# Decoder layer, one core: the experts' first norm moved into cross attention, x2 stored a batch later, the experts' steps reordered

## The reference

```
x = layernorm(x + self_attention(x, relative position bias))
x = layernorm(x + cross_attention(x, ctx, ctx))
x = layernorm(x + ffn(x))
ffn: aff = x @ centroids.T (8 experts); e = argmax(aff); alpha = sigmoid(aff[e])
     h  = relu((layernorm(x) * g[e] + b[e]) @ w1[e].T + b1[e])   # 256 -> 1024
     ye = x + h @ w2[e].T + b2[e];   out = alpha * ye + (1 - alpha) * x
```

## Time and profile before

| | us |
|---|---|
| median of 3 runs (lowest, highest) | 1068.13 (1065.26, 1069.1) |
| the profiled execution: its time | 1071.02 |
| its span, first to last instruction | 1069.2 |
| PE, ACT, DVE, POOL busy over the span | 942.3, 772.8, 675.9, 347.9 |
| mean granted TensorE clock | 0.937 of full |

### The profile page before, as it was taken

How to read it: one execution, slowest core, us unless ns; L and a number is a source line. 1 busy time by engine, 2 the same in 40 slices (tenths; PEclk the granted TensorE clock), 3 DMA queues, 4 the chain that set the end, 5 groups by cost and what they waited for, 6 DMA issues and landing times. The chain is left out here.

```text
span 1069.2 us, 17528 instructions
## 1 busy us (share of the span) xinstructions
PE 942.3 (88%) x5301; PEld 523.5 (49%) x5301; DVE 675.9 (63%) x1760; ACT 772.8 (72%) x1452; POOL 347.9 (33%) x340
## 2 busy tenths in 40 slices
PE   5599999999999999999999999962599889898891
PEld 2233444444444433333333333321599779888790
DVE  5276877777777777354546464753377667667672
ACT  1387777787877868899989898940478767686670
POOL 4043133140313111001112211221436666665664
PEclk9699999999999989999999999985699999898895
DMA  8988587978769576695587558400523334333441
GB/s 210 201 229 235 120 249 143 320 153 243 201 154 275 103 195 109 148 266 110 123 151 153 105 117 160 100 20 28 197 91 119 105 110 176 105 117 115 127 169 44
DMA packets 73546, 162.93 MB, mean 152 GB/s; under 512 B 16441, under 2 KB 40056, under 8 KB 63416
## 3 DMA queue, kind: packets, MB, share of 16 engines
q1 hardware_dynamic: 68088, 152.23, 56.5%
q0 software_dynamic: 5056, 9.20, 3.0%
q10 hardware_dynamic: 320, 0.52, 0.1%
HBM read 116.40 MB, written 49.54 MB: 155 GB/s over the span
## 5 line engine op out<-in xcount | busy, mean ns | idle before, releaser
L717 ACT ACTIVATE probs<-sc 128x512 f32<-128x512 f32 x1024 | 528.5, 607 | 110.6 <-DVE sc L799 82.7
L491 PE MATMUL sc<-qst,kst 57*128 57x512 f32 (+1 forms) x1024 | 269.5, 471 | 18.0 <-DMA qst<-s_qk 12.4
L799 DVE TENSOR_TENSOR sc<-sc,strip 128x308 f32<-128x308 f32 (+1 forms) x512 | 192.9, 429 | 101.7 <-PE sc L491 100.8
L503 PE MATMUL ot<-probs,vals 128*32 128x512 f32 x1600 | 215.0, 610 | 0.0
L491 PEld LDWEIGHTS sc<-qst,kst 57*128 57x128 f32 (+1 forms) x1024 | 118.1, 186 | 193.0 <-ACT probs L717 147.9
L1753 POOL DMA_INDIRECT f_rows<-s_x,f_get_ids x45 | 107.0, 2378 | 36.4 <-issue 34.8
L1611 ACT ACTIVATE f_h<-f_h_ps,f_par 128x384 f32<-128x384 f32 x104 | 64.0, 616 | 27.0 <-PE f_h_ps L1530 26.9
L1691 DVE TENSOR_TENSOR f_h_lo<-f_h,f_h_hi 128x384 fp32r<-128x384 f32 x104 | 56.9, 547 | 27.8 <-ACT f_h_hi L1612 27.4
L1189 POOL TENSOR_SCALAR veps<-mv_self 128x4 f32<-128x4 f32 x8 | 1.9, 232 | 192.3 <-DVE mv_self L857 192.3
L1612 ACT ACTIVATE f_h_hi<-f_h_ps,f_par 128x384 fp32r<-128x384 f32 x104 | 64.3, 618 | 0.0
L1252 POOL DMA_INDIRECT s_tokens<-ids,place_i x32 | 32.9, 1029 | 88.9 <-DVE place_i L943 81.6
(11 more groups left out here) (173 smaller groups left out, 1672.8 us busy)
## 6 DMA issues: line engine op xcount, KB each, us to landing
s_qk<-w_hi SPq DMA_DIRECT2D x32, 512.0 KB, 7.1
strip<-in_w_all SPq DMA_DIRECT2D x16, 1024.0 KB, 11.8
f_raw<-in_w_all SPq DMA_DIRECT2D x14, 1024.0 KB
kst<-s_qk SPq DMA_DIRECT2D x32, 256.0 KB, 6.1
qst<-s_qk SPq DMA_DIRECT2D x32, 256.0 KB, 7.4
s_x_parts<-split SPq DMA_DIRECT2D x16, 512.0 KB, 8.6
kst<-s_ctx_parts SPq DMA_DIRECT2D x32, 256.0 KB, 6.1
qst<-s_x_parts SPq DMA_DIRECT2D x32, 256.0 KB, 7.3
```

Source lines behind the costliest of these rows:

```text
L491: nc.tensor.matmul(sc[j][:], kst[at:at + rows, i, P * c:P * c + P], qst[at:at + rows, i, :], start=True, stop=True).then_inc(scored, 1)
L503: last = nc.tensor.matmul(sums_bank(n, g)[32 * j:32 * j + 32, :], vals[:, c, 4 * g + j, :], probs[:, k % KEPT, j, :], start=(c == 0), stop ...
L717: nc.scalar.activation(probs[:, k % KEPT, j, :], sc[j][:], ACT.Exp, scale=scale).then_inc(exped, 1)
L799: nc.vector.tensor_tensor(sc[j][:, lo:hi], sc[j][:, lo:hi], band_backwards(rank_of(4 * g + j), at, hi - lo), ALU.add).then_inc(biased, 1)
```

## The change

1. **First norm in cross attention.** The experts' first norm is taken of x2 while cross attention runs: `stats_of_x2` at k 9 and 10, `inverse_deviation_h` on POOL, `hat_x2` at k 14. The row in memory is now x2, the weight and the normed x2, 513 floats. `norm_in`, `hat_in` and one `rstd_of` leave the experts' steps; `turn_in` transposes the gathered rows themselves.
2. **Stores.** `store_x2(c - 2)` stands ahead of `load_x1(c)` in the next body; before, `store_x2(c - 1)` stood between the two halves of the pair loads.
3. **End of the last batch**, in four pieces of 128 tokens: norm, transposes, copy (now ACT's) and affinities of a piece follow its add. The last list scatter and the last x2 store stand behind the soundness branch.
4. **Boundary.** First parameters and the first two get lists are loaded at the end of the first part, into buffers that both parts share; the small clearing block is gone, so is the second clearing of the row buffers (now in cross body 1) and the second load of `ident`.
5. **Experts' step.** ACT makes the plain relu only; DVE makes the high half as a copy and the low half behind it (`split_h`). Weight halves are made in pieces of 1024 columns at f 0, 1, 3, 4 (ACT) and f 1, 2, 5, 7 (DVE). ACT takes over the last norm's final scaling (`hat_out`, f 7), DVE the epsilon. POOL: gather first, then `keep_rows` (copy of 3 x 257 columns), one power, scatter. SP: the put list last.
6. **Last tile.** Turned, gated, added, normed and scattered in three pieces; POOL drains once ahead of its powers (`finish`).

The core of the diff:

```diff
-ROW = C + 1
+ROW = 2 * C + 1
@@ sync, cross_body @@
+                if c > 1:
+                    store_x2(c - 2)
                 load_x1(c)
@@ tensor, after the last body @@
+            for t in range(3):
+                turn_out(B - 1, t)
+            turn_x2_last(0)
+            turn_out(B - 1, 3)
+            turn_x2_last(1)
             for t in range(NC):
-                turn_out(B - 1, t)
+                if t + 2 < NC:
+                    turn_x2_last(t + 2)
+                affinities_last(t)
@@ vector @@
+            def hat_x2(c):
+                dve.wait_ge(h_rstd, c + 1)
+                for t in range(NC):
+                    last = nc.vector.tensor_scalar(x2[:, t, C + 1:ROW], x2[:, t, 0:C], mv_h[:, t, 0:1], rstd_h[:, t:t + 1], ALU.subtract, ALU.mult)
+                last.then_inc(have_hat, 1)
...
+                    if k == 9:
+                        stats_of_x2(c - 1, range(0, 2))
+                    if k == 10:
+                        stats_of_x2(c - 1, range(2, NC))
+                    if k == 14:
+                        hat_x2(c - 1)
@@ end of the first part, sync @@
+            store_last(sp)
+            sp.dma_start(par[0][:], io["params"][0]).then_inc(early["ld_par0"], 16)
+            sp.wait_ge(st_last_ids, 16 * NC)
+            sp.wait_ge(pstep, 15)
+            for i in range(2):
+                first_list = sp.value_load(plan[0:1, 1, i:i + 1], min_val=0, max_val=E * FULL_LIST - 1)
+                sp.dma_start(get_ids[i][:], ...).then_inc(early["ld_get"][i], 16)
+            sp.wait_ge(st_x2, 16 * B)
@@ experts, scalar @@
                 nc.scalar.activation(h[f % (LAG + 1)][:], h_ps[f % (LAG + 1)][:], ACT.Relu, bias=bias).then_inc(h_full, 1)
-                nc.scalar.activation(h_hi[f % (LAG + 1)][:], h_ps[f % (LAG + 1)][:], ACT.Relu, bias=bias).then_inc(h_hi_ready, 1)
@@ experts, vector @@
+            def split_h(i, f):
+                at = f % (LAG + 1)
+                dve.wait_ge(h_full, FC * i + f + 1)
+                wait(dve, y_mm, FC * i + f - LAG)
+                nc.vector.tensor_copy(h_hi[at][:], h[at][:]).then_inc(h_hi_ready, 1)
+                wait(dve, h_hi_ready, FC * i + f + 1, dve_passed)
+                nc.vector.tensor_tensor(h_lo[at][:], h[at][:], h_hi[at][:].bitcast(F32), ALU.subtract).then_inc(h_ready, 1)
@@ experts, gpsimd @@
             def step(i, s, n):
-                rstd_of(i + 1, mv_in, mv_in_ready, veps_in, rstd_in, have_xhat, have_rstd_in)
-                if not isinstance(i, int) or i > 0:
-                    rstd_of(i - 1, mv_out, mv_out_ready, veps_out, rstd_out, have_out, have_rstd_out)
                 gather(i + 2, s, n + 1)
-                if not isinstance(i, int) or i > 0:
-                    scatter(i - 1)
+                keep_rows(i + 1, 1 - s, n + s)
+                if later(i):
+                    inverse_deviation(i - 1)
+                    scatter_rows(i - 1)
+            def finish(i):
+                pool.drain()
+                for t in range(TC):
+                    wait(pool, veps_out, i + t + 1, pool_passed)
...
```

More of the change, by code:

```diff
@@ L1455, in tiles, with later @@
             return count
+        def later(i):
+            return not isinstance(i, int) or i > 0
         list_of = scratch["tokens"].rearrange("(l p n) o -> l p (n o)", p=P, n=TC * STEP)
@@ new lines, in hat_last, with step @@
+            def hat_last(i, t):
+                dve.wait_ge(have_rstd_out, i + t + 1)
+                if t == 0:
+                    wait(dve, st_out, 16 * TC * i)
+                nc.vector.tensor_scalar(normed[:, t, :], res[:, t, :], mv_out[:, t, 0:1], rstd_out[:, t:t + 1],
+                                        ALU.subtract, ALU.mult).then_inc(have_out, 1)
+            def step(i, s, n):
+                for f in range(FC):
+                    split_h(i, f)
+                    if f in (1, 2):
+                        low_w(i + 1, 1 - s, 0, f - 1, w1_lo_ready)
+                    if later(i) and f == 3:
+                        add_rows(i - 1, 1 - s)
+                    if later(i) and f == 4:
+                        norm_out(i - 1)
+                    if f in (5, 7):
+                        low_w(i + 1, 1 - s, 1, f // 7, w2_lo_ready)
+                    if f == 6:
+                        if later(i):
+                            shift_rows(i - 1)
+                        low_in(i + 1, 1 - s)
```

455 lines of the change are left out of this document (252 added, 203 removed).

## The result

The changed kernel takes 1049.52 us (median of 4 runs, 1047.07 to 1051.86), the kernel before 1068.25 (4 runs); ratio 0.984, 95% interval 0.980 to 0.987. The forecast was 1011 in a range of 1000 to 1033: right in its direction, wrong in its size. The profiled execution of the changed kernel took 1047.07 us with a span of 1045.2; against 1069.2 before that is 24.0 us less, where the working had 57.3 (the medians differ by 18.7; executions of one kernel lie some us apart).

| part | before | after | forecast | measured |
|---|---|---|---|---|
| A, to the first expert matmul | 762.55 | 762.63 | -10.5 | +0.1 |
| B, from there to the first kept y | 20.5 | 22.8 | +1 | +2.3 |
| C, twelve periods | 260.7 | 239.3 | -41.2 | -21.4 |
| D, from the last kept y to the end | 25.4 | 20.5 | -6.6 | -4.9 |

The account below looks back on a forecast made before the run. No engine was full: PE's waits on DVE's order made the 21.73 us period. From the profiled span, -10.5 (to first expert matmul), +1 (first tile), -41.2 (twelve periods), -6.6 (end) sum to -57.3: 1011 us, range 1000 to 1033.

Parts of the forecast that it names:

- about 0.4 ahead of its `ffn2`: Expert tile: DVE's last split of h is done about 0.4 us before PE's matmul needs it.
- The 0.5 us added for disturbance: Expert tile: POOL and DVE disturb each other, so 0.5 us a tile is added to the period.
- PE's own work: Expert tile: 96 matmuls and twelve transposes, 16.6 + 1.2 = 17.8 us, taken as the lower bound of the period.
- the 18.3 of the forecast: Twelve expert periods: 18.3 us each, down from 21.73, which gives -41.2 us.
- The first rival: Expert tiles: POOL becomes the bound, PE waits 1 to 2 us a tile; period 19.8, 1029 us; chance 0.24.
- Cost at nothing: Cross bodies: +1.8 us statistics and +1.4 hat on DVE, hidden beside ACT's exponentials; 3.6 us of cover for x2.
- The second rival: Cross bodies: bigger x2 store lands late, PE stops 1.5 to 2 us in six bodies; +10, 1021 us; chance 0.08.
- The four scalings ahead of the last batch: Last batch: batch 6's four scalings stand ahead of its sums on DVE, so it starts 1.4 us late.
- only the x2 store waits: Last batch: batch 7's hat, behind the places, delays only the x2 store, and the scatter's chain is longer.
- third rival: Expert tiles: DVE starves POOL's scatters and gathers; slower, 1079 us at a period of 24; chance 0.04.
- costs nothing: End: POOL's drain lies beside a longer wait, since the put list ends last, so it adds nothing.
- y + 6.7: End: last scatter from 6.7 us behind the last kept y, against 13.35 before; -6.6 us.

Follow-up runs that it names:

- low_w_last: Changed kernel with both low halves of W2 taken behind split_h(7), no longer behind split_h(5) and split_h(7): 1033.46 us, ratio 0.971 to the kernel before.
- high_on_act: Changed kernel with the high part of h made by ACT as a second relu, DVE left with the subtraction: 1035.89 us, ratio 0.973 to the kernel before.
- keep_on_act: Changed kernel with the copy of the kept rows on ACT behind relu(6), none on POOL: 1033.66 us, ratio 0.971 to the kernel before.
- combined: Changed kernel with x2 stored at its body's end, W2 low halves last, kept rows copied by ACT, last list ahead of the branch, no drain: 1017.65 us, 0.956.
- the early store: Changed kernel with x2 of batch c-1 stored at the end of body c, no longer in body c+1: 1038.10 us, ratio 0.976 to the kernel before.
- best2: `best` with the second tile's weights asked for behind the first tile's gathers: 1002.88 us, ratio 0.942 to the kernel before.
- list_early: Changed kernel with the last batch's token list written by POOL ahead of its branch on the soundness test: 1050.62 us, ratio 0.985 to the kernel before.
- weights_after_first: Changed kernel with the second tile's weights asked for once the first tile's gathers have landed, not both tiles': 1043.83 us, ratio 0.978 to the kernel before.
- no_drain: Changed kernel without POOL's drain ahead of the last tile's norm: 1050.18 us, ratio 0.984 to the kernel before.
- list_and_store: Changed kernel with the last token list ahead of the branch and the last x2 store in two, normed columns earlier: 1043.50 us, ratio 0.978.
- best: Changed kernel with early x2 store, W2 low halves last, kept rows on ACT, early list, last x2 store in two, drain in every tile: 1009.02 us, 0.943.

## Why the prediction was wrong

**C, 19.8 of the missing 33.3 us.** The step that failed is the sentence that the last `split_h` stands "about 0.4 ahead of its `ffn2`". PE waited 0.67 us for it, and 0.66 for the one before it; the forecast had no row and no sum behind its 0.4. The forecast summed DVE's busy time (15.0; measured 15.96) and compared it with the period, as if only a full engine could be late. But its run of 17.8 us began at the first relu, some 2 us into the tile, since the relu stands behind `keep_y` (1.05 us) and then waits 0.23 us for PE; what counts is when that run reaches blocks 6 and 7. The 0.5 us added for disturbance was mis-sized: it is 1.16. PE's own work is 18.06 and not 17.8, the two waits are 1.88 in place of the 0.5: 19.94. `low_w_last`, `high_on_act` and `keep_on_act` each gave 1.1 to 1.3 us a tile back, and the two of them that went into `combined` brought the period to 18.06, below the 18.3 of the forecast. So waits on PE, no slower PE, made the difference. The first rival had nearly this period (19.8), for the wrong reason: POOL's DMAs were at 1.2 us, inside what the forecast gave them.

**A, 10.6 us.** The turned rows came 8.4 us later and not 1.4: 7.0. The step that failed is "Cost at nothing", which left the store's landing out. The second rival came true at its size, by luck: it had +10 from PE stopping 1.5 to 2 us in six bodies, and the early store gave back 9.8; but the bodies that grew are three, by 4.0, 1.7 and 6.0 us, the last with a fallen clock that the rival didn't have. The four scalings ahead of the last batch, 1.4 us in the forecast, cost nothing (56.3 us before and now). The forecast gave this rival 0.08 and put it aside, though the rows that decide it were at hand: issue 6 us later, cover 3.6 us, and twice the bytes to land. Its chance should have been worked out from these, not felt. The new order of the last batch brought less than was forecast: choice is 15.6 us behind the turned rows and was 17.9, so -2.3, where the forecast's sum has 13.9 (712.15 to 726.05), so -4.0. Its first norm stands 1.70 us in a wait that the sum doesn't have:

```profile
726.65 0.41 DVE L931 TENSOR_SCALAR x<-xr,mv,rstd 128x256 f32<-128x256 f32 x1 [1.70 <-DMA s_x<-x]
```

In `best2` this norm waits 1.32 us for POOL's power instead, and choice is 15.2 us behind the turned rows, so the store of batch 6 explains at most 0.4 of the 1.7; the rest stays open. From the places on, the branch and the 1 MB store each held the gather for 2.4 us more than it takes without both (14.0 and 11.6 us). The sentence that "only the x2 store waits" for the last hat "and the scatter's chain is longer than the store" was a failed step too: in `list_early`, with the same store, the list could be read only 6.3 us behind its last scatter, with half the store 3.9; and that the list now stands behind the branch (last scatter 7.2 us behind the places, before 4.9) was put at nothing. What was saved behind the places and what was lost ahead of them hid each other in the first matmul, 762.63 against 762.55. Of the 10.6 us, 7.0 are the turned rows, 1.7 the way to choice and 2.4 the branch; behind the last list scatter 0.4 came back.

**B, 1.3 us.** The mechanism was right (weights asked for beside the first matmul), the size 2.3 and not 1; `weights_after_first` gives 2.4 back.

**D, 1.7 us.** That the drain "costs nothing" was wrong by its place, 6.98 us ahead of the power, and right in the sum, since the end of the program takes what the drain doesn't. The forecast knew neither; it had the end behind the scatter as a constant of 12.0 us from the earlier trace rows, and that fell to 6.3. Without the drain the first of the last scatters was at y + 8.4 (`no_drain`), still not at y + 6.7.

**Right**: clock 1.00 in all twelve periods (the reason given for it is too simple: in the kernel before the clock fell behind stops of PE of 1.41 and 1.53 us, at 875.12 and 877.96, but not behind 0.71 and 2.27, at 851.02 and 854.60), POOL's DMAs hardly disturbed (1.19 us), no starvation (third rival), the added statistics hidden in the changed kernel, the sign.

## What to carry to other kernels

An engine with a fifth of its time idle can still set the period: look at where its run of work stands when the last consumer asks, not at its sum. A store that grows and moves back in its queue needs both distances written down, issue to landing and issue to the next writer, in every body, and a late one can cost more than its wait where the clock falls with it. And when an experiment that takes a wait away shows nothing, look for a second chain that ends at the same place, or for the same time at the program's end, before calling the wait free.

## What the runs showed of the hardware

- POOL's fp32 copy of 128x771 (0.83 us) lengthened the one two-input instruction of DVE beside it from 0.56 to 1.72 us, more than the copy's own length. ACT doing the same copy lengthened none (mean 558 ns).
- A list of 512 ids, four small indirect DMAs, could be read 6.3 and 6.0 us behind its last DMA where a 1 MB store had been issued 2.8 us ahead of that DMA (`list_early`, `combined`), and 3.9 and 4.0 us behind it with half a megabyte (`list_and_store`, `best2`). Rows gathered beside 2 MB of weights took 9.5 us to PE and not 6.5.
- Behind many indirect DMAs of GpSimd some 6 us appear once: 6.98 us at a drain ahead of the last norms, or the span ends 9.4 and 9.6 us behind the last scatter's start and not 3.6 (before, `no_drain`). One drain ahead of the tiles leaves 9.1; with one in every tile they appear nowhere. What is finished there isn't shown.
- The granted clock fell from 2.4 to 1.2 GHz in one cross body in every trace with the late store (from 632 to 645 in the changed kernel), behind a stop of PE of 3.71 us; in `best` it fell in a cross body without a stop ahead of it.
